# Cross scores of 18 batches in a fused cross-attention and expert block: float32 products against products of high and low halves

## The chip, the core and the metric

One Trainium2 chip, of which the kernel uses one core: TensorE (matrix products, PE in the profile), VectorE (DVE), ScalarE (ACT), GpSimd (POOL) and SyncE (SP, which issues the transfers), with 16 DMA engines. The metric is the time of one execution on the device in microseconds; the kernel before has a median of 1141.99 us of 3 runs (1141.2 to 1142.24).

## What is computed

Tokens x (8 x 112 x 512) pass a gated attention block and then a gated block of experts. The attention has queries in 16 heads of 128 channels and 8 groups of keys and values, once over the tokens themselves ("self") and once over 375 rows of context a batch ("cross"). Cut to the cross part:

```python
qx = _fp8_linear_pertensor(ln_out, wqx, wqx_scale, qx_in_scale).reshape(b, s, g, hpg, d)
qx = _ln(qx, qxln_w, qxln_b)
kvx = jnp.einsum('bsi,oi->bso', cond, w_kv_x)
kx, vx = jnp.split(kvx, 2, axis=-1)
kx = _ln(kx.reshape(b, sc, g, d), kxln_w, kxln_b)
xout = _gqa(qx, kx, vx).reshape(b, s, nh * d)      # softmax(qx kx^T * scale) vx
cat = jnp.concatenate([core, xout], axis=-1)       # core: the self part
```

cat is rounded to 8-bit floats and projected, added to x, and the experts follow. Everything is in float32, to float32's accuracy but for the roundings to 8 bits.

## The kernel before

The attention runs in four groups (gp = 0 to 3), each of 4 query heads (HP) and 2 key heads (HD = 128 channels each), and in each group over the 8 batches, so there are 32 batches (g, u). Projections of queries and own keys are made for 7 tiles of 128 tokens (TJ), those of the context for each batch. A step (s, t) projects for position s (project 0 to 5: queries, cross queries, own keys and values, and three chunks of 125 context rows) and at the same time works off the attention of the batch t before it. The order of every engine is written out by hand in its step function (ScalarE near line 713, TensorE near line 905, VectorE near line 1165), and each engine runs its instructions in that order; semaphores tie them together. The steps between two positions with a tile, (g, 0) to (g, 6), are all alike; (g, 7) has last_step.

For batch t, TensorE runs after turn(t, 3) (the first key head of the context, transposed into bank p_cross[1]): project(s, 2), score_self(t) (line 836), score_cross(t, 0) and (t, 1) (line 843), turn(t, 4) (the second key head, into p_tr[1]), project(s, 3) (line 799), turn_self (850), turn_cross(t, 0) (857, which writes p_tr[1] too), score_cross(t, 2), turn_cross(t, 1), score_cross(t, 3), project(s, 4), outputs(t, 0), turn_cross 2 and 3, project(s, 5), outputs(t, 1). ScalarE copies the transposed queries and keys out of PSUM with weight and bias (turned, lines 641 to 649: qxT, kxT), and makes exp_self (657) and exp_cross (665). VectorE finds the maxima (max_self 1094, max_cross 1108), divides by the sums (norm_self 1102, norm_cross 1114 and 1116), and copies transposed probabilities (take_self 1122, take_cross 1127). smoothed (1134) writes the result into y[t % 2]; Results.exponents and rounded (201 to 212) round it and put it into a buffer cat, which SP stores to memory (store); rounded waits for the store before it.

A cross score is one product in float32, keys of 375 rows against queries of 112:

```python
pe.matmul(p_cross[0:T, h % 2, 0:TC], qxT[:, t[1] % 2, h, :], kxT[:, h // HPG, :],
          start=True, stop=True).then_inc(sx_rdy, 1)
```

In the trace each such product is two instructions. The projections, by contrast, are already made of float32r halves (x_hi = x in float32r, x_lo = x - x_hi; hi*hi + lo*hi + hi*lo).

## Time and profile before

| | |
|---|---|
| median of 3 runs | 1141.99 us |
| the profiled execution | 1142.36 us |
| its span, first to last instruction | 1140.6 us |
| TensorE busy | 1085.6 us, 95% |
| VectorE busy | 775.2 us, 68% |
| ScalarE busy | 697.9 us, 61% |
| GpSimd busy | 500.9 us, 44% |
| attention stage | to about 788 us |

Busy times overlap between engines. A TensorE instruction's length in the trace includes the time until its result has left the array, so the lengths of neighbours overlap and what one costs is the distance from its start to the next one's. A batch is named (g, u), from 0; its times are given from the start of its score_self.

### The profile page before, as it was taken

To read this page: it belongs to the slowest core of one execution; us is meant where nothing else is said; L and a number is where in the kernel's file an instruction comes from. 1 tells how busy PE (TensorE), PEld (TensorE's weight loads), DVE (VectorE), ACT (ScalarE), POOL (GpSimd) and SP (SyncE) were. 2 spreads that over 40 slices of the span, in tenths; PEclk is the share of its full clock that TensorE was granted. 3 is DMA by queue.
4 is the path that set the end of the run, shared out by engine and by line. 5 is a ranking of instruction groups with operands and counts; after the bars stand their busy time and mean duration, and the time that the engine had idled before them with its cause. 6 is when DMAs were issued, how large, how long until landed. Compare 5 with 4: busy or idle time off the path is not lost. (4 is left out here: it accounts for less than half of the span.)

```text
span 1140.6 us, 19544 instructions
## 1 busy us (share of the span) xinstructions
PE 1085.6 (95%) x5681; PEld 896.1 (79%) x5681; DVE 775.2 (68%) x1569; ACT 697.9 (61%) x2034; POOL 500.9 (44%) x576
## 2 busy tenths in 40 slices
PE   4599999999999999999999999998999789999996
PEld 3488888888888888888888888886888667878885
DVE  7999986977776887777697766667454884655000
ACT  7668888776878856888877656762241324434432
POOL 3446565445445454545544544542000235555432
PEclk8799999999999999999999999999999889999999
DMA  7221111142111214111114111112954357673310
GB/s 267 95 81 47 51 39 43 36 170 77 43 36 47 60 35 185 47 52 38 43 36 154 48 42 40 42 35 95 333 164 163 130 160 213 187 238 96 54 43 0
DMA packets 52819, 107.39 MB, mean 94 GB/s; under 512 B 6064, under 2 KB 27056, under 8 KB 51184
## 3 DMA queue, kind: packets, MB, share of 16 engines
q1 hardware_dynamic: 48016, 97.00, 25.8%
q0 software_dynamic: 4704, 9.18, 3.6%
q8 instruction: 49, 0.80, 0.3%
q14 instruction: 50, 0.41, 0.1%
HBM read 91.48 MB, written 16.52 MB: 95 GB/s over the span
## 5 line engine op out<-in xcount | busy, mean ns | idle before, releaser
L529 POOL TENSOR_TENSOR c_lo<-c_raw,c_hi 128x500 fp32r<-128x500 f32 x96 | 123.0, 1282 | 193.0 <-ACT c_hi L582 171.4
L523 POOL TENSOR_TENSOR rs<-va,mhalf 125x2 f32<-125x2 f32 (+1 forms) x180 | 201.5, 1119 | 14.2 <-POOL va L516 0.2
L516 POOL TENSOR_TENSOR va<-ss,epst 125x2 f32<-125x2 f32 (+1 forms) x180 | 59.4, 330 | 175.0 <-DVE ss L1079 100.6
L799 PE MATMUL bank<-w_hi,c_hi 128*125 128x512 f32 x384 | 120.1, 434 | 8.9 <-ACT w_hi L577 8.0
L772 PE MATMUL bank<-w_hi,xqs 128*128 128x512 f32 (+2 forms) x464 | 111.1, 362 | 11.2 <-DVE xqs L1071 11.2
L799 PE MATMUL bank<-w_lo,c_hi 128*125 128x512 f32 x384 | 105.7, 396 | 0.1
L799 PE MATMUL bank<-w_hi,c_lo 128*125 128x512 f32 x384 | 105.3, 396 | 0.0
L772 PE MATMUL bank<-w_lo,xqs 128*128 128x512 f32 (+2 forms) x464 | 101.3, 340 | 0.1
L665 ACT ACTIVATE work<-bank,nmax 112x375 f32<-112x375 f32 x128 | 73.5, 587 | 44.2 <-DVE nmax L1108 43.9
L843 PE MATMUL bank<-kxT,qxT 128*112 128x375 f32 x256 | 96.9, 480 | 0.0
L799 PEld LDWEIGHTS bank<-w_hi,c_hi 128*125 128x125 f32 x384 | 67.0, 188 | 27.1 <-issue 8.2
L772 PEld LDWEIGHTS bank<-w_hi,xqs 128*128 128x128 f32 (+1 forms) x464 | 73.7, 189 | 17.7 <-issue 11.8
L799 PEld LDWEIGHTS bank<-w_lo,c_hi 128*125 128x125 f32 x384 | 71.5, 186 | 18.9 <-DVE w_lo L434 0.8
L799 PEld LDWEIGHTS bank<-w_hi,c_lo 128*125 128x125 f32 x384 | 71.6, 186 | 18.6
L772 PEld LDWEIGHTS bank<-w_lo,xqs 128*128 128x128 f32 (+1 forms) x464 | 75.6, 187 | 11.4 <-DVE w_lo L434 0.8
L874 PE MATMUL bank<-work 125*128 125x224 f32 x384 | 83.1, 352 | 0.0
L874 PEld LDWEIGHTS bank<-work 125*128 125x128 f32 x384 | 72.5, 189 | 0.3
L627 ACT ACTIVATE nkx<-bank 125x256 f32<-125x256 f32 x96 | 38.8, 404 | 55.4 <-PE bank L799 55.4
L1134 DVE TENSOR_TENSOR results<-bank,smg 128x448 bf16<-128x448 f32 x64 | 39.8, 622 | 46.1 <-PE bank L874 45.9
L1108 DVE TENSOR_REDUCE nmax<-bank 112x1 f32<-112x375 f32 x128 | 69.2, 543 | 2.7 <-PE bank L843 0.2
L1524 POOL DMA_INDIRECT out<-p_cat,of_row x21 | 43.6, 2075 | 58.9 <-ACT p_cat L1628 45.9
L582 ACT ACTIVATE c_hi<-c_raw 128x500 fp32r<-128x500 f32 x96 | 64.1, 668 | 1.5 <-DMA c_raw<-in_ctxT 1.5
(274 smaller groups left out, 2790.8 us busy)
## 6 DMA issues: line engine op xcount, KB each, us to landing
c_raw<-in_ctxT SPq DMA_DIRECT2D x96, 250.0 KB, 2.6
shared<-in_w_in SPq DMA_DIRECT2D x13, 1024.0 KB, 8.9
shared<-in_wproj SPq DMA_DIRECT2D x32, 256.0 KB, 4.1
raw_g<-in_Wg SPq DMA_DIRECT2D x8, 1024.0 KB, 6.5
raw_u<-in_Wu SPq DMA_DIRECT2D x8, 1024.0 KB, 6.1
raw_d<-in_Wd SPq DMA_DIRECT2D x8, 1024.0 KB, 5.5
cat_scratch<-results SPq DMA_DIRECT2D x32, 224.0 KB, 2.0
shared<-cat_scratch SPq DMA_DIRECT2D x2, 1792.0 KB, 9.9
```

The costliest lines, as they stand in the source:

```text
L516: pool.tensor_tensor(va[0:rows, lo:hi], ss[0:rows, lo:hi], epst[0:rows, lo:hi], ALU.add).then_inc(va_done, 1)
L523: pool.tensor_tensor(rs[0:rows, lo:hi], va[0:rows, lo:hi], mhalf[0:rows, lo:hi], ALU.pow).then_inc(rs_done, 1)
L529: pool.tensor_tensor(flat(c_lo[:, k, :, :]), flat(c_raw[:, k, :, :]), flat(c_hi[:, k, :, :]).bitcast(F32), ALU.subtract).then_inc(cl_done, 1)
L582: act.activation(flat(c_hi[:, k, :, :]), flat(c_raw[:, k, :, :]), ACT.Copy).then_inc(ch_done, 1)
L665: act.activation(pcross[0:T, h, :], p_cross[0:T, h % 2, 0:TC], ACT.Exp, bias=nmax[0:T, 4 + h:5 + h], accum_out=lsum[0:T, 4 + h:5 + h]).the ...
L772: m = pe.matmul(out, xqs[:, n, k, 0:rows], (w_hi, w_lo)[i // KB][:, k, lo:lo + w], start=(i == 0), stop=(i == 2 * KB - 1))
L799: m = pe.matmul(bank[0:CT, :], a[:, ch, k, :], w[:, k, CKX:CV], start=(i == 0), stop=(i == 3 * KB - 1))
L843: pe.matmul(p_cross[0:T, h % 2, 0:TC], qxT[:, t[1] % 2, h, :], kxT[:, h // HPG, :], start=True, stop=True).then_inc(sx_rdy, 1)
L874: m = pe.matmul(out[:, HPG * T:2 * HPG * T], valx[0:CT, par, k, g * P:(g + 1) * P], flat(pcrossT[0:CT, k, HPG * g:HPG * (g + 1), :]), star ...
L1108: v.tensor_reduce(nmax[0:T, 4 + h:5 + h], p_cross[0:T, h % 2, 0:TC], AX, ALU.max, negate=True).then_inc(mx_done, 1)
L1134: v.tensor_tensor(results.y[lin(t) % 2][:, g * 4 * T:(g + 1) * 4 * T].rearrange("p (a t) -> p a t", t=T), out_bank(t, g)[:, 0:4 * T].rearr ...
L1524: pool.indirect_dma_start(out=tokens[:, :], out_offset=bass.IndirectOffsetOnAxis(ap=of_row[:, 1, i:i + 1], axis=0), in_=y[:, i % 2, :], in ...
```

## The change

For the 18 batches (g, u) with g > 0 and u < 6 (has_halves), each cross score is made of three float32r products instead of one in float32: queries' low by keys' high, high by high, and queries' high by keys' low half, all into one PSUM tile; 375 columns become 376 (one of zeros). The halves are made by VectorE, with six new instructions a batch: a copy and a subtraction for the four heads' queries (halves_of_queries), and for each of two key heads a multiply-and-add straight out of the PSUM bank into kx_hi and a subtraction from kxT into kx_lo (halves_of_keys). halves_of_queries and halves_of_keys(t, 0) stand ahead of max_self, halves_of_keys(t, 1) behind norm_cross 1. TensorE's order of the steps is kept; score_cross waits for the halves, and turn_cross(t, 0), which writes the bank from which kx_hi of the second head is made, waits for that as well.

To make room, kxT has one key head instead of two (turned(t, 4) now waits for score_cross 1), pcross two heads instead of four, the results have no buffer of their own for the rounded value (the subtraction is in place, and smoothed waits for the store of two batches before), and small tiles share memory. In the last step, without projections, TensorE's turn(t, 4) moves behind the cross scores, and so does ScalarE's turned(t, 4). SP's loop over batches is unrolled.

```diff
@@ Results
-        self.held = sb(c, "results", [P, 4 * 8 * T], BF16)
-        *self.y, self.e, self.cat = (self.held[:, k * 8 * T:(k + 1) * 8 * T] for k in range(4))
+        self.held = sb(c, "results", [P, 6 * FF], BF16)
+        *self.y, self.e = (self.held[:, k * 8 * T:(k + 1) * 8 * T] for k in range(3))
+        self.rest = self.held[:, 3 * 8 * T:6 * FF]
...
-        v.wait_ge(self.stored, 16 * (t + 1))
-        v.tensor_tensor(self.cat[:, :], y[:, :], self.e[:, :], ALU.subtract).then_inc(self.ct_done, 1)
+        v.tensor_tensor(y[:, :], y[:, :], self.e[:, :], ALU.subtract).then_inc(self.ct_done, 1)
...
+def has_halves(pos):
+    return pos[0] > 0 and pos[1] < TJ - 1
+def halves_no(pos, n):
+    return 6 * ((TJ - 1) * (pos[0] - 1) + pos[1]) + n + 1
...
-    kxT = sb(c, "kxT", [P, 2, TC])
+    kxT = sb(c, "kxT", [P, TC + 1])
+    qx_hi = sb(c, "qx_hi", [P, HP, T], F32R)
+    qx_lo = sb(c, "qx_lo", [P, HP, T], F32R)
+    kx_hi = sb(c, "kx_hi", [P, TC + 1], F32R)
+    kx_lo = sb(c, "kx_lo", [P, TC + 1], F32R)
@@ SyncE
-            with sp.Fori(2, B) as b:
+            for b in range(2, B):
@@ ScalarE, turned
             if n >= 3:
-                act.activation(kxT[:, n - 3, :], turn_bank(n)[:, 0:TC], ACT.Identity, bias=b,
+                if n == 4:
+                    act.wait_ge(sx_rdy, 4 * (lin(t) + 1) + 2)
+                act.activation(kxT[:, 0:TC], turn_bank(n)[:, 0:TC], ACT.Identity, bias=b,
                                scale=w).then_inc(t_done, 1)
@@ ScalarE, exp_cross
-            act.wait_ge(tr_rdy, tr_no(before(t), 6 + h))
+            act.wait_ge(tr_rdy, tr_no(before(t), 8 + h) if h < 2 else tr_no(t, 4 + h))
@@ TensorE, bank_free
+            elif n == 6 and has_halves(t):
+                pe.wait_ge(t_done, td_no(t, 4))
+                pe.wait_ge(halves, halves_no(t, 4))
@@ TensorE, score_cross
-            pe.matmul(p_cross[0:T, h % 2, 0:TC], qxT[:, t[1] % 2, h, :], kxT[:, h // HPG, :],
-                      start=True, stop=True).then_inc(sx_rdy, 1)
+            out, kh = p_cross[0:T, h % 2, 0:TC + 1], h // HPG
+            if not has_halves(t):
+                pe.matmul(out[:, 0:TC], qxT[:, t[1] % 2, h, :], kxT[:, 0:TC], start=True, stop=True).then_inc(sx_rdy, 1)
+                return
+            pe.wait_ge(halves, halves_no(t, 2 + 2 * kh))
+            pe.matmul(out, qx_lo[:, h, :], kx_hi[:, :], start=True, stop=False)
+            pe.matmul(out, qx_hi[:, h, :], kx_hi[:, :], start=False, stop=False)
+            pe.wait_ge(halves, halves_no(t, 3 + 2 * kh))
+            pe.matmul(out, qx_hi[:, h, :], kx_lo[:, :], start=False, stop=True).then_inc(sx_rdy, 1)
@@ TensorE, step
-            if not A: turn(t, 4)
-            if not A: score_self(t)
             if A: project(s, 2, g)
-            if A and Q: score_self(t)
+            if Q: score_self(t)
             if Q: score_cross(t, 0)
             if Q: score_cross(t, 1)
-            if A and Q: turn(t, 4)
+            if Q: turn(t, 4)
@@ VectorE
+        def halves_of_queries(t):
+            if not has_halves(t):
+                return
+            whole = flat(qxT[:, t[1] % 2, :, :])
+            v.wait_ge(t_done, td_no(t, 1))
+            v.wait_ge(sx_rdy, 4 * lin(t) + 4)
+            v.tensor_copy(flat(qx_hi[:, :, :]), whole).then_inc(halves, 1)
+            v.wait_ge(halves, halves_no(t, 0))
+            v.tensor_tensor(flat(qx_lo[:, :, :]), whole, flat(qx_hi[:, :, :]).bitcast(F32),
+                            ALU.subtract).then_inc(halves, 1)
+        def halves_of_keys(t, kh):
+            if not has_halves(t):
+                return
+            v.wait_ge(t_done, td_no(t, 3 + kh))
+            v.wait_ge(sx_rdy, 4 * lin(t) + 4 + 2 * kh)
+            v.tensor_scalar(kx_hi[:, 0:TC], turn_bank(3 + kh)[:, 0:TC], vec[:, V_KXW:V_KXW + 1],
+                            vec[:, V_KXB:V_KXB + 1], ALU.mult, ALU.add).then_inc(halves, 1)
+            v.wait_ge(halves, halves_no(t, 2 + 2 * kh))
+            v.tensor_tensor(kx_lo[:, :], kxT[:, :], kx_hi[:, :].bitcast(F32), ALU.subtract).then_inc(halves, 1)
@@ VectorE, smoothed
             if lin(t) > 1:
-                v.wait_ge(results.ct_done, lin(t) - 1)
+                v.wait_ge(results.stored, 16 * lin(t))
@@ VectorE, step
+            if Q: halves_of_queries(t)
+            if Q: halves_of_keys(t, 0)
             if Q: max_self(t)
             if Q: max_cross(t, 0)
             if Q: max_cross(t, 1)
...
             if Q: norm_self(t)
             if Q: norm_cross(t, 0)
             if Q: norm_cross(t, 1)
+            if Q: halves_of_keys(t, 1)
             if spread: rounding(s[1] + 2, 0, 2, 2)
             if Q: take_self(t)
```

## Rows read from the trace of the kernel before

**Rows 1.** The page's first part: busy time, share of the span and instructions of each engine.
```profile
PE 1085.6 (95%) x5681; PEld 896.1 (79%) x5681; DVE 775.2 (68%) x1569; ACT 697.9 (61%) x2034; POOL 500.9 (44%) x576
```

**Rows 2.** Waits of TensorE from 240 to 750 us: engine, line, releaser, total, times, longest.
```profile
PE bank L857 <- DVE work L1116: 0.6, 2, 0.3
```

**Rows 3.** Windows of one step each: busy time and instructions by engine, clock, DMA share, GB/s.
```profile
505.86:529.63 23.77, 23.77 (x134) 20.06 (x133) 18.00 (x39) 19.90 (x67) 11.64 (x16) 1.00 0.16 44
715.03:738.80 23.77, 23.77 (x135) 20.06 (x134) 16.26 (x37) 15.32 (x54) 11.56 (x16) 1.00 0.16 43
```

**Rows 4.** Timeline of TensorE in one step: start, length, line, output and inputs, count.
```profile
505.86 0.94 PE L836 MATMUL bank<-kT,qT 128*112 128x112 f32 x8
506.65 1.43 PE L843 MATMUL bank<-kxT,qxT 128*112 128x375 f32 x4
...
509.16 1.08 PE L799 MATMUL bank<-w_hi,c_lo 128*125 128x512 f32 x4
510.09 1.09 PE L799 MATMUL bank<-w_lo,c_hi 128*125 128x512 f32 x4
...
511.40 0.49 PE L857 MATMUL bank<-ident,work 112*125 112x112 f32 x3
511.73 0.80 PE L843 MATMUL bank<-kxT,qxT 128*112 128x375 f32 x2
512.36 0.48 PE L857 MATMUL bank<-ident,work 112*125 112x112 f32 x3
```

**Rows 5.** Timeline of ScalarE in the same step.
```profile
503.63 0.59 ACT L649 ACTIVATE qxT<-bank,vec 128x256 f32<-128x256 f32 x1
...
505.28 0.71 ACT L641 ACTIVATE kxT<-bank,vec 128x375 f32<-128x375 f32 x1
...
506.78 0.69 ACT L582 ACTIVATE c_hi<-c_raw 128x500 fp32r<-128x500 f32 x1
507.50 0.35 ACT L657 ACTIVATE pself<-bank,nmax 112x112 f32<-112x112 f32 x1
...
509.84 0.23 ACT L665 ACTIVATION_READ_ACCUMULATOR work<-bank,nmax 112x1 f32 x1
509.93 0.69 ACT L641 ACTIVATE kxT<-bank,vec 128x375 f32<-128x375 f32 x1
```

**Rows 6.** Timeline of VectorE in the same step.
```profile
504.15 0.68 DVE L1079 TENSOR_REDUCE ss<-sq 128x4 f32<-128x512 f32 x1
506.85 0.62 DVE L1094 TENSOR_REDUCE nmax<-bank 112x4 f32<-112x448 f32 x1 [2.02 <-PE bank L836]
...
510.10 0.17 DVE L1114 RECIPROCAL linv<-lsum 112x2 f32<-112x2 f32 x1 [0.28 <-ACT work L665]
510.30 0.74 DVE L1116 TENSOR_SCALAR work<-work,linv 112x375 f32<-112x375 f32 x2
511.60 0.62 DVE L1122 COPY pselfT<-bank 112x448 f32<-112x448 f32 x1 [0.56 <-PE bank L850]
...
517.81 0.62 DVE L1134 TENSOR_TENSOR results<-bank,smg 128x448 bf16<-128x448 f32 x1 [0.29 <-PE bank L874]
```

**Rows 7.** VectorE's instructions: groups by line and form, 240 to 745 us; L1116 in this step.
```profile
L1127 DVE COPY work<-bank 125x336 f32<-125x336 f32 x84 | 40.1, 498 | 0.7 <-PE bank L857 0.7
...
L1088 DVE TENSOR_TENSOR nkx<-nkx,rs 125x256 f32<-125x256 f32 x66 | 26.8, 416 | 0.2
...
L1102 DVE TENSOR_TENSOR pself<-pself,linv 112x448 f32<-112x448 f32 x22 | 13.7, 625 | 0.8
...
L1116 DVE TENSOR_SCALAR work<-work,linv x4: 402/412/508, 510.3 to 516.5; 112x375 f32<-112x375 f32 x4
```

**Rows 8.** Timelines of VectorE, then TensorE, in batch 7 of group 2.
```profile
601.16 0.74 DVE L1116 TENSOR_SCALAR work<-work,linv 112x375 f32<-112x375 f32 x2
...
601.64 0.58 PE L857 MATMUL bank<-ident,work 112*125 112x112 f32 x3 [0.29 <-DVE work L1116]
602.05 0.80 PE L843 MATMUL bank<-kxT,qxT 128*112 128x375 f32 x2
```

More of the change, by code:

```diff
@@ L210, in rounded @@
         v.wait_ge(self.rnd, 3 * t + 3)
-        v.wait_ge(self.stored, 16 * (t + 1))
-        v.tensor_tensor(self.cat[:, :], y[:, :], self.e[:, :], ALU.subtract).then_inc(self.ct_done, 1)
+        v.tensor_tensor(y[:, :], y[:, :], self.e[:, :], ALU.subtract).then_inc(self.ct_done, 1)
     def store(self, sp, t):
         sp.wait_ge(self.ct_done, t + 1)
-        sp.dma_start(self.catd[t], self.cat[:, :]).then_inc(self.stored, 16)
+        sp.dma_start(self.catd[t], self.y[t % 2][:, :]).then_inc(self.stored, 16)
 def normed_rows(shared):
@@ L314, in attention @@
     sq = sb(c, "sq", [P, 2, 512])
-    sqx = sb(c, "sqx", [P, 2 * HD], BF16)
+    sqx = results.rest[:, 0:2 * HD]
     re = sb(c, "re", [P, 4, 2, P], BF16)
-    st = sb(c, "st", [P, TJ, 6])
     mv = sb(c, "mv", [P, TJ, 2])
@@ L323, in attention @@
     xof = sb(c, "xof", [P, 4, KB])
-    smr = sb(c, "smr", [P, GP, 8])
-    work = sb(c, "work", [P, HP * TC + 2 * NC * 256 + NC * HP * T])
-    pcross = work[:, 0:HP * TC].rearrange("p (h c) -> p h c", h=HP)
-    at = HP * TC
+    work = sb(c, "work", [P, 2 * TC + 2 * NC * 256 + NC * HP * T])
+    pcross = work[:, 0:2 * TC].rearrange("p (h c) -> p h c", h=2)
+    at = 2 * TC
     valx = work[:, at:at + 2 * NC * 256].rearrange("p (a k n) -> p a k n", a=2, k=NC)
@@ L331, in attention @@
     xs = work[:, 0:TJ * D].rearrange("p (j d) -> p j d", j=TJ)
-    ss = sb(c, "ss", [P, 16])
-    va = sb(c, "va", [P, 16])
-    rs = sb(c, "rs", [P, 16])
+    st = work[:, TJ * D:TJ * D + TJ * 6].rearrange("p (j n) -> p j n", j=TJ)
+    ss, va, rs = (results.rest[:, 2 * HD + 32 * n:2 * HD + 32 * (n + 1)].bitcast(F32) for n in range(3))
     qT = sb(c, "qT", [P, 2, HP, T])
@@ L390, in attention @@
     sx_rdy = sem(c, "sx_rdy")
+    halves = sem(c, "cross_halves")
     mx_done = sem(c, "mx_done")
@@ L455, in _ @@
         sp.dma_start(scal[:, :], scalars.partition_broadcast(P)).then_inc(vec_in, 16)
-        sp.dma_start(smr[:, :, :], smooth).then_inc(vec_in, 16)
+        sp.dma_start(smi[:, :, :], smooth).then_inc(vec_in, 16)
         for j in range(1, TJ):
@@ L496, in _ @@
         pool.memset(epst[:, :], EPS).then_inc(pool_self, 1)
+        pool.memset(kxT[:, TC:TC + 1], 0.0).then_inc(const_done, 1)
         pool.wait_ge(pool_self, 3)
@@ L662, in exp_cross @@
             act.wait_ge(mx_done, 4 * (lin(t) + 1) + h + 1)
-            act.wait_ge(tr_rdy, tr_no(before(t), 6 + h))
+            act.wait_ge(tr_rdy, tr_no(before(t), 8 + h) if h < 2 else tr_no(t, 4 + h))
             act.wait_ge(nx_done, 4 * lin(t) + h + 1)
-            act.activation(pcross[0:T, h, :], p_cross[0:T, h % 2, 0:TC], ACT.Exp,
+            act.activation(pcross[0:T, h % 2, :], p_cross[0:T, h % 2, 0:TC], ACT.Exp,
                            bias=nmax[0:T, 4 + h:5 + h], accum_out=lsum[0:T, 4 + h:5 + h]).then_inc(ex_done, 1)
@@ L707, in step @@
             if Q: turned(t, 3)
-            if not A and Q: turned(t, 4)
             if A: take(s, 1)
@@ L713, in step @@
             if Q: exp_cross(t, 1)
-            if A and Q: turned(t, 4)
+            if Q: turned(t, 4)
             if A: take(s, 2)
@@ L856, in turn_cross @@
             for k in range(NC):
-                m = pe.transpose(p_tr[0:CT, 1 - h % 2, k * T:(k + 1) * T], pcross[0:T, h, k * CT:(k + 1) * CT],
+                m = pe.transpose(p_tr[0:CT, 1 - h % 2, k * T:(k + 1) * T], pcross[0:T, h % 2, k * CT:(k + 1) * CT],
                                  ident[0:T, 0:T])
@@ L938, in step @@
             if Q: outputs(t, 1)
-        pe.wait_ge(const_done, 1)
+        pe.wait_ge(const_done, 2)
         for j in range(TJ):
@@ L1025, in constants @@
         def constants():
-            link(v.reciprocal(smi[:, :, :], smr[:, :, :]))
+            link(v.reciprocal(smi[:, :, :], smi[:, :, :]))
             for col in (V_KW, V_KB, V_KXW, V_KXB):
@@ L1115, in norm_cross @@
                 v.wait_ge(dv, CH * lin(t) + 2 + h // 2)
-            v.tensor_scalar(pcross[0:T, h, :], pcross[0:T, h, :], linv[0:T, 4 + h:5 + h], None,
+            v.tensor_scalar(pcross[0:T, h % 2, :], pcross[0:T, h % 2, :], linv[0:T, 4 + h:5 + h], None,
                             ALU.mult).then_inc(nx_done, 1)
@@ L1231, in step @@
                 inputs((s[0], s[1] + 1))
+                v.wait_ge(const_done, 2)
+                v.tensor_copy(kx_hi[:, TC:TC + 1], kxT[:, TC:TC + 1])
                 constants()
```

## The prediction

> **What bounds the kernel now.** The page's first part says that TensorE is busy 95% of the span [rows 1]. The waits of TensorE, between 240 us (just ahead of the first changed batch) and 750 us (behind the last changed scores), hold only two, 0.6 us together, and neither lies in a changed batch [rows 2]. A window over one step (23.77 us between two score_self) shows TensorE busy for all of it at a granted clock of 1.00, VectorE for 18.00, ScalarE for 19.90; a late step has the same length though VectorE and ScalarE do less [rows 3]. So TensorE's instructions set the step, and a microsecond more or less of them is a microsecond of the kernel, as long as what they wait for is there in time. Whether it is, I read from the timelines of the three engines in one step, that of batch 3 of group 2. Times below are counted from the start of its score_self, 505.86 [rows 4].
>
> **What is removed.** One head's cross scores are two instructions of 375 columns and take 0.63 us (511.73 to 512.36) [rows 4]. They become three in float32r with 376 columns. The nearest rows are c_lo's four float32r products of 512 columns, 0.93 us from one group's start to the next, 0.2325 us each [rows 4]; by columns, 0.171 us for 376, 0.512 for three. (Spacing is the price, not the duration: neighbours overlap.) Gain: 0.118 us a head, 0.47 us for four, and 72 heads would give 8.5 us if nothing waited. The lower bound of the price is half of an old instruction's 0.315, 0.158 us: then 0.475 us for three.
> The Trainium skill (TensorE: Matmul & The Clock Gate, Back-to-back issue gap) gives columns/2.4 + 2.5 ns for a matmul at full clock. That would be 0.159 us for 376 columns; its 0.216 for 512 columns is less than the 0.2325 that the trace shows for float32r, so the row is taken.
>
> **What is added, and where it waits.** Six VectorE instructions a batch. Prices by neighbours: from PSUM, 336 elements take 0.498 us, so 375 about 0.54 (keys' high half); a two-operand product in SBUF takes 0.416 for 256 and 0.625 for 448, so 376 about 0.54 (keys' low half) and 448 0.62 (queries' low half); the queries' copy is near the 0.41 of a one-operand 375, at most 0.62 [rows 7]. Together some 3.2 us, on 18.00 of 23.77 [rows 3]: VectorE isn't the bound, but its order matters.
> - *Queries.* ScalarE has written qxT at -1.64 [rows 5] and VectorE is through with sums(s, 0) at -1.03 [rows 6]. Copy and subtraction end at about 0.1 even at 0.62 each. Cost nothing: keys aren't there sooner.
> - *Keys, first head.* kxT ends at 0.13 (505.28 + 0.71) [rows 5]. With 0.03 us for each hand-over (exp_cross 1 ends at 509.84 + 0.23, the reciprocal that waits for it starts at 510.10 [rows 5, 6]) the high half runs 0.16 to 0.70, the low half 0.73 to 1.27. score_cross 0 starts at 0.79 [rows 4]: its first two products find what they need, its third, due at 1.13, waits until about 1.31. Of the 0.24 gained by heads 0 and 1 some 0.2 is lost there. That costs nothing by itself, for a longer wait follows.
> - *max_self* is queued behind the two. It started at 0.99 [rows 6]; a VectorE instruction that waits for nothing starts some 0.08 us before its predecessor's end (at 510.30 two products take 0.74 together, of 0.41 each [rows 6, 7]), so now at 1.19. exp_self started at 1.64, just when both max_self and ScalarE's work before were done; so all of exp_self, exp_cross 0 and 1, turned 4 comes 0.20 later, and norm_cross 1 ends at 5.38 in place of 5.18 [rows 5, 6].
> - *Keys, second head*, are queued behind norm_cross 1. kxT is written at 4.76 + 0.20 = 4.96 [rows 5], so they wait for VectorE alone: high half 5.30 to 5.84, low half 5.87 to 6.41. But turn_cross 0 overwrites that PSUM bank and now waits for the high half. It started at 5.54 [rows 4]; in batch 7 of group 2, where the same transposes did wait, they started 0.07 after norm_cross 0 (601.16 + 0.41; they start at 601.64), and head 2's scores 0.41 after them, not 0.33 as here [rows 4, 8]. So turn_cross 0 starts at 5.91 (0.37 late), score_cross 2 at 6.32 in place of 5.87 (0.45 late). TensorE can't fill the gap: its instructions are in order, and behind this one are all the others of the step.
> - *From there* the low half is in time (6.44 against 6.66), and heads 2 and 3 give back 2 x 0.118 = 0.24. Net **+0.21 us a step**.
> - *What is late next.* take_self waited for TensorE and started at 5.74 [rows 6]; now VectorE is through with the low half at 6.33, so the chain down to max_cross 3 is 0.6 late. It has no deadline before outputs 0 and turn_cross 2, more than 0.5 us on; before smoothed(t, 0) VectorE had 0.29 us idle [rows 6], TensorE itself is 0.2 later, and of its 5.8 idle us a step [rows 3] more lie behind. Nothing is carried to the next step.
>
> **The rest costs nothing.** One kxT in place of two: turned 4 comes after exp_cross 1, which needs score_cross 1 anyway. Two pcross in place of four: exp_cross 2 needs score_cross 2, which TensorE runs behind turn_cross 0; head 3 likewise. The results' own buffer gone: the wait for the store moves from the subtraction to smoothed two batches later, a whole step after the store; SP issues that store behind the loads of c_raw as before, unrolled or not. If its cover were gone, smoothed, and outputs behind it, would wait for a store of 224 KB. The constants' edits lie ahead of TensorE's first instruction or beside it. At the last batch turn 4 moves behind the cross scores, but head 2 waits for norm_cross 0 there too.
>
> **Sum.** 18 steps x 0.21 = +3.8 us against the profiled execution's 1142.36 (span 1140.6 and 1.76 around it): 1146.2 us. That execution is 0.37 above the median, so the median goes from 1141.99 to **1145.8 us**.
>
> **Bounds.** Each high half may take 0.41 (the one-operand SBUF row) to 0.62 us; two of them are in the path: -0.26 to +0.16 a step. The three products per head at the lower bound: -0.08 for heads 2 and 3. The restart's 0.08 may be absent. The ends are -0.21 and +0.37 a step, 1138.2 and 1148.7; the high one with subtractions at 0.62 too is 1150.
>
> **Rivals.**
> 1. *VectorE's reads of the bank are cheap.* With 0.41 us for each high half turn_cross 0 starts 0.26 sooner and the step ends 0.05 before the old one: 1141.1 us. For it: VectorE's multiply in SBUF takes that. Against it: the copy out of PSUM takes 0.498 us for 336 elements, the multiply 0.41 for 375 [rows 7].
> 2. *The other side: the wait is hidden.* If the second head's high half is visible by 5.46, when TensorE gets there, all four heads' gain stays: 72 x 0.118 = 8.5 us, 1133.5. It turns faster once the high half ends before about 5.63, 0.21 sooner than I have it. Against it: norm_cross 1, ahead of it on VectorE, alone ends at 5.18 now, and 0.5 us must follow.
> 3. *The plain rate.* At 0.158 us a product the stall stays and heads 2 and 3 give 0.31: +0.14 a step, 1144.4. The Trainium skill's gap rule, cited above, is this case.
> 4. *More is lost.* All new instructions at 0.62 us, or a second restart in the middle of score_cross 0 that delays max_cross: +0.44 a step, 1149.9.
>
> **Chances.** Forecast 0.55 (1143.5 to 1148), rival 1 0.17, rival 2 0.08, rival 3 0.12, rival 4 0.08. About 0.2% (2.3 us) is what can be told from no change: below 1139.7 is faster, above 1144.3 slower. Slower: 0.48 of the forecast, 0.07 of rival 3, rival 4: 0.63. Faster: rival 2 and 0.05 of rival 1: 0.13. Same: 0.24. The range from 1140 to 1149 leaves out rival 2, part of rival 1 and half of rival 4, some 0.17.
>
> **What the changed profile would show.** score_cross with 376 columns spaced 0.17; turn_cross 0 the top row of TensorE's waits, 18 times, on VectorE's high half, about 0.3 us idle each; TensorE's step 23.98 in place of 23.77 in 18 steps and the same in the others; exp_self 0.2 later; VectorE some 58 us busier. Wrong would be: no wait at turn_cross 0 (rival 2), high halves of 0.4 us (rival 1), steps longer by 0.4 (rival 4), or a change outside the 18 steps.

## The result: 1152.95 us, and the profile after

The changed kernel takes 1152.95 us (median of four runs, 1151.78 to 1155.17), the one before, run beside it, 1141.6 (1141.08 to 1142.24). The ratio is 1.0093 [1.0081, 1.0106]: slower by some 11 us. The forecast, 1145.8 with 1140 to 1149, has the side right and the size too small: the measured time lies outside the range. The profiled execution took 1152.14 us with a span of 1150.4, against 1142.36 and 1140.6 before: 9.8 us more.

The page's first part for the kernel after answers to [rows 1]:
```profile
PE 1089.2 (95%) x5753; PEld 908.7 (79%) x5753; DVE 831.8 (72%) x1678; ACT 698.8 (61%) x2034; POOL 511.8 (44%) x577
```
VectorE is 56.6 us busier (775.2 to 831.8; forecast 58), ScalarE does what it did.

The waits of TensorE between 240 and 760 us (engine, what waits, releaser: total, times, longest) answer to [rows 2]:
```profile
PE bank L882 <- DVE kx_hi L1132: 6.3, 18, 0.4
```
This row is new. It is the wait that the prediction named: turn_cross 0 (L882) on the keys' high half (L1132), once in each of the 18 changed batches, 0.35 us each.

A window of one step in group 2 (from one score_self to the next; length, busy time of TensorE, its weight loads, VectorE, ScalarE and GpSimd, granted clock) answers to [rows 3]:
```profile
510.06:534.39 24.33, 23.94 (x139) 20.74 (x138) 21.06 (x45) 19.92 (x67) 12.28 (x16) 1.00 0.16 42
```
From one score_self to the next it takes 24.33 us in place of 23.77; all 18 changed batches are longer by about as much, to a few hundredths, and the other steps are as before (23.75 for 23.77 in group 0). 18 x 0.56 = 10.1 us, which is the whole difference of the profiled executions (9.8). The forecast was 0.21 a step. So 0.35 us a step had to be found. The clock is 1.00 in this step on both sides and has no part in it.

The timelines of TensorE, then VectorE, in batch 3 of group 2, from score_self at 510.06 (start, length, engine, line, operation, count, and in brackets the idle time before and its releaser), answer to [rows 4] and [rows 6]:
```profile
510.06 0.95 PE L854 MATMUL bank<-kT,qT 128*112 128x112 f32 x8
511.04 0.39 PE L866 MATMUL bank<-kx_hi,qx_lo 128*112 128x376 f32 x1
511.27 0.33 PE L867 MATMUL bank<-kx_hi,qx_hi 128*112 128x376 f32 x1
511.56 0.43 PE L869 MATMUL bank<-kx_lo,qx_hi 128*112 128x376 f32 x1
511.82 0.34 PE L866 MATMUL bank<-kx_hi,qx_lo 128*112 128x376 f32 x1
512.00 0.33 PE L867 MATMUL bank<-kx_hi,qx_hi 128*112 128x376 f32 x1
512.17 0.33 PE L869 MATMUL bank<-kx_lo,qx_hi 128*112 128x376 f32 x1
...
516.33 0.55 PE L882 MATMUL bank<-ident,work 112*125 112x112 f32 x3 [0.35 <-DVE kx_hi L1132]
516.65 0.40 PE L866 MATMUL bank<-kx_hi,qx_lo 128*112 128x376 f32 x1
...
518.07 1.10 PE L814 MATMUL bank<-w_hi,c_hi 128*125 128x512 f32 x4
```
```profile
508.94 0.38 DVE L1121 CAST qx_hi<-qxT 128x448 fp32r<-128x448 f32 x1
509.36 0.62 DVE L1123 TENSOR_TENSOR qx_lo<-qxT,qx_hi 128x448 fp32r<-128x448 f32 x1
510.23 0.67 DVE L1132 TENSOR_SCALAR kx_hi<-bank,vec 128x375 fp32r<-128x375 f32 x1 [0.24 <-ACT kxT L657]
510.93 0.57 DVE L1135 TENSOR_TENSOR kx_lo<-kxT,kx_hi 128x376 fp32r<-128x376 f32 x1
511.43 0.61 DVE L1140 TENSOR_REDUCE nmax<-bank 112x4 f32<-112x448 f32 x1
...
514.87 0.74 DVE L1162 TENSOR_SCALAR work<-work,linv 112x375 f32<-112x375 f32 x2
515.53 0.66 DVE L1132 TENSOR_SCALAR kx_hi<-bank,vec 128x375 fp32r<-128x375 f32 x1
516.22 0.55 DVE L1135 TENSOR_TENSOR kx_lo<-kxT,kx_hi 128x376 fp32r<-128x376 f32 x1
```
Put beside the forecast, all counted from score_self:

| | forecast | after |
|---|---|---|
| distance of two products | 0.171 | 0.17 to 0.18 |
| keys' high half, first head | 0.16 to 0.70 | 0.17 to 0.84 |
| keys' low half, first head, ends | 1.27 | 1.44 |
| max_self starts | 1.19 | 1.37 |
| norm_cross 1 ends | 5.38 | 5.55 |
| keys' high half, second head | 5.30 to 5.84 | 5.47 to 6.13 |
| from its end to turn_cross 0 | 0.07 | 0.14 |
| turn_cross 0 starts | 5.91 | 6.27 |
| project after the four heads | 7.66 | 8.01 |

The forecast for project is its start before, 7.45 (the group behind it starts at 8.38, less 0.93 for its own four products), plus 0.21. The missing time is three terms: 0.17 from the first head's halves, handed on unchanged to norm_cross 1; 0.12 because the second high half takes 0.66 and not 0.54; 0.07 in the hand-over. Together 0.36 at turn_cross 0, and no more and no less behind it. The trace says where; it does not say why a high half takes 0.66, nor whether the first head's low half could have ended sooner. On the latter there is a row that the prediction never looked at, GpSimd's low half of the tokens, c_low (L529 before, L543 after), first in the kernel before, then after:
```profile
505.51 1.25 POOL L529 TENSOR_TENSOR c_lo<-c_raw,c_hi 128x500 fp32r<-128x500 f32 x1 [5.46 <-ACT c_hi L582]
```
```profile
509.71 1.38 POOL L543 TENSOR_TENSOR c_lo<-c_raw,c_hi 128x500 fp32r<-128x500 f32 x1 [4.98 <-ACT c_hi L596]
```
It runs from -0.35 to 0.90 before and from -0.35 to 1.03 after, right through the keys' first high half. In the changed kernel it takes 1.38 us in eight of the 18 batches and 1.26 in the other ten. The eight are those in which the queries' low half still runs when it starts (here 509.36 to 509.98, c_low at 509.71); in the ten that half is through at -0.54. In those ten (625.82 in group 3, for one) the keys' first low half takes 0.60 and ends at 1.47, the second high half ends at 6.16 and turn_cross 0 starts at 6.30: 0.03 later than in the eight. A short GpSimd addition, begun at 0.87, runs beside the start of that low half.

### The profile page after: what moved, and what is told of

Its sections match the earlier page's. It is cut to its first block and busy times, and to the rows that moved or that the text cites. A ratio compares the mean times of both kernels' runs of the same rounds, so it can differ in the third digit from the quotient of the medians.

```text
span 1150.4 us, 19476 instructions
## 1 busy us (share of the span) xinstructions
PE 1089.2 (95%) x5753; PEld 908.7 (79%) x5753; DVE 831.8 (72%) x1678; ACT 698.8 (61%) x2034; POOL 511.8 (44%) x577
## 5 line engine op out<-in xcount | busy, mean ns | idle before, releaser
L537 POOL TENSOR_TENSOR results<-results,mhalf 125x2 f32<-125x2 f32 (+1 forms) x180 | 202.2, 1123 | 14.1
L543 POOL TENSOR_TENSOR c_lo<-c_raw,c_hi 128x500 fp32r<-128x500 f32 x96 | 124.3, 1295 | 188.2 <-ACT c_hi L596 166.6
L530 POOL TENSOR_TENSOR results<-results,epst 125x2 f32<-125x2 f32 (+1 forms) x180 | 64.9, 361 | 181.8 <-DVE results L1102 111.2
L814 PE MATMUL bank<-w_hi,c_hi 128*125 128x512 f32 x384 | 114.4, 420 | 8.3 <-ACT w_hi L591 7.4
L1575 POOL DMA_INDIRECT out<-p_cat,of_row x21 | 46.2, 2199 | 58.5 <-ACT p_cat L1679 47.9
L882 PEld LDWEIGHTS bank<-ident,work 112*125 112x125 f32 x384 | 53.7, 188 | 17.1 <-issue 9.7
L882 PE MATMUL bank<-ident,work 112*125 112x112 f32 x384 | 58.8, 275 | 7.6 <-DVE kx_hi L1132 6.3
```

Source lines behind the costliest of these rows:

```text
L530: pool.tensor_tensor(va[0:rows, lo:hi], ss[0:rows, lo:hi], epst[0:rows, lo:hi], ALU.add).then_inc(va_done, 1)
L537: pool.tensor_tensor(rs[0:rows, lo:hi], va[0:rows, lo:hi], mhalf[0:rows, lo:hi], ALU.pow).then_inc(rs_done, 1)
L543: pool.tensor_tensor(flat(c_lo[:, k, :, :]), flat(c_raw[:, k, :, :]), flat(c_hi[:, k, :, :]).bitcast(F32), ALU.subtract).then_inc(cl_done, 1)
L814: m = pe.matmul(bank[0:CT, :], a[:, ch, k, :], w[:, k, CKX:CV], start=(i == 0), stop=(i == 3 * KB - 1))
L882: m = pe.transpose(p_tr[0:CT, 1 - h % 2, k * T:(k + 1) * T], pcross[0:T, h % 2, k * CT:(k + 1) * CT], ident[0:T, 0:T])
L1575: pool.indirect_dma_start(out=tokens[:, :], out_offset=bass.IndirectOffsetOnAxis(ap=of_row[:, 1, i:i + 1], axis=0), in_=y[:, i % 2, :], in ...
```

## The experiments

All edits are to the changed kernel. Steps are those of group 2 unless said otherwise. Two theories were to be told apart at first: the high halves are dear because of where they read (the PSUM bank, with weight and bias as operands), or because of what they run beside (GpSimd).

**The high half as a copy of the written kxT, e1_copy and e2_copy_wait.** Both read kxT in SBUF. The first also drops turn_cross 0's wait, since the bank is free once ScalarE has written kxT; the second keeps it.
```
-            elif n == 6 and has_halves(t):                      (e1_copy alone)
-                pe.wait_ge(t_done, td_no(t, 4))
-                pe.wait_ge(halves, halves_no(t, 4))
...
-            v.tensor_scalar(kx_hi[:, 0:TC], turn_bank(3 + kh)[:, 0:TC], vec[:, V_KXW:V_KXW + 1],
-                            vec[:, V_KXB:V_KXB + 1], ALU.mult, ALU.add).then_inc(halves, 1)
+            v.tensor_copy(kx_hi[:, 0:TC], kxT[:, 0:TC]).then_inc(halves, 1)
```


> Edit: the keys' high half is a copy of kxT in SBUF instead of a multiply-and-add out of the PSUM bank, and turn_cross 0 no longer waits for it (only for ScalarE's kxT, as before the change). Theory A (the high half out of the bank costs 0.66 us where 0.54 was forecast, stands twice in the path, and turn_cross 0 waits for its end): the copy takes about 0.35 us (448 elements take 0.39), max_self starts at about 1.05 instead of 1.37 after score_self, norm_cross 1 ends at about 5.25, turn_cross 0 doesn't wait; score_cross 2 finds both halves about in time. The step falls from 24.33 us to 23.35-23.5, below the 23.77 of the kernel before; 1134 to 1137 us. Rival B (the cost is on TensorE: three products with their own weight loads and semaphore waits are no cheaper than two in float32): the step stays above 24.1, 1148 us or more. Rival C (the smaller buffers or the moved wait for the store cost): the same, above 1148.

> Edit: the high half is a copy of kxT as in e1, but turn_cross 0 still waits for it. Separates the price of the high half from the wait itself. Theory A: the second high half ends at about 5.25 - 0.08 + 0.35 = 5.52 after score_self, turn_cross 0 starts at about 5.6 to 5.65 instead of 6.27 (it would start at 5.35 without any wait), so the step is 23.6 to 23.75 and the time 1139 to 1142 us: most of the loss is the price, the wait is worth another 3 to 6 us. Rivals B and C: above 1148 us.

Measured: e1_copy 1148.83 us, ratio to the kernel before 1.0067 [1.0045, 1.009], step 24.25; e2_copy_wait 1154.46, 1.0109 [1.0092, 1.0126], step 24.38. Both forecasts missed, and both times lie where rivals B and C would put them, so the time alone doesn't decide; the rows do, and e5_buffers and e8_stale_keys below. The top wait of TensorE in e1_copy has moved from turn_cross 0 to the first product of score_cross 0:
```profile
PE bank L863 <- DVE kx_hi L1129: 6.8, 18, 0.5
```
VectorE and GpSimd in e1_copy, score_self at 509.63:
```profile
509.80 1.08 DVE L1129 CAST kx_hi<-kxT 128x375 fp32r<-128x375 f32 x1 [0.25 <-ACT kxT L657]
...
515.48 0.35 DVE L1129 CAST kx_hi<-kxT 128x375 fp32r<-128x375 f32 x1
```
```profile
509.28 1.38 POOL L543 TENSOR_TENSOR c_lo<-c_raw,c_hi 128x500 fp32r<-128x500 f32 x1 [4.71 <-ACT c_hi L596]
```
The same instruction takes 0.35 us for the second head and 1.08 for the first. The first one begins while c_low runs; 0.35 before its end is 510.53, 0.13 before c_low's recorded end at 510.66. It was held until GpSimd was all but through and then ran at its own speed. In the batches whose c_low takes 1.26 the copy takes 0.96: the same 0.12 less. The Trainium skill (SBUF — State Buffer, Who interferes with whom) states such a thing: VectorE shares one pair of ports with GpSimd and contends for it by a copy, a cast or a tensor_scalar in its two-port mode, or by an instruction with two SBUF inputs while GpSimd reads SBUF; the engine that issues first keeps it for its whole instruction and the other is blocked. This trace agrees, but for the 0.13 us by which the copy was ahead of c_low's recorded end. So the SBUF source is cheap (0.35 against 0.66) and the gain is lost again where it meets c_low. The wait at turn_cross 0 in itself is worth 0.13 a step (24.38 against 24.25), and that was the smaller part of the loss. In e2_copy_wait TensorE waits 6.7 us at score_cross 0 as well, and the second high half ends at 6.20, later than the 6.13 of the changed kernel, although it is the shorter instruction.

**Six forms of the high half, e3_forms.** One for each group and head, to price operand and source. Where weight or bias is missing, the high half is of other numbers, and the products lose accuracy alone, since the low half makes up the rest.
```
+            form = (t[0], kh)
+            if form == (1, 0): ins = v.tensor_scalar(dst, src, w, None, ALU.mult)
+            elif form == (1, 1): ins = v.tensor_scalar(dst, src, 0.5, 0.25, ALU.mult, ALU.add)
+            elif form == (2, 0): ins = v.tensor_copy(dst, src)
+            elif form == (2, 1): ins = v.tensor_scalar(dst, kxT[:, 0:TC], w, b, ALU.mult, ALU.add)
+            elif form == (3, 0): ins = v.tensor_scalar(dst, kxT[:, 0:TC], w, None, ALU.mult)
+            else: ins = v.tensor_scalar(..., w, b, ALU.mult, ALU.add)      (bank, 374 columns)
```


> A look at what makes the high half 0.66 us. Its form differs by group and key head (the scores are then of wrong keys' high halves in all 18 batches; low halves are the rest, so the sums of halves still differ from the keys only where the high half isn't rounded right): group 1 head 0 from the bank with one pointer scalar; group 1 head 1 from the bank with two constants; group 2 head 0 a plain copy from the bank; group 2 head 1 from kxT in SBUF with two pointers; group 3 head 0 from kxT with one pointer; group 3 head 1 from the bank with two pointers and 374 columns. If the two pointer scalars are dear: 0.54 for one pointer, constants and copy from the bank, and 374 columns stay at 0.66. If the bank as source with an odd count is dear: 374 columns 0.54. If the rounding to float32r is dear: all from the bank 0.66, and the SBUF forms above 0.41.

Measured: 1149.51 us (one run). The groups of VectorE's instructions by form (busy us, mean ns of one | idle before):
```profile
L1139 DVE TENSOR_SCALAR kx_hi<-kxT,vec 128x375 fp32r<-128x375 f32 x6 | 5.7, 955 | 4.3 <-ACT kxT L657 4.3
L1140 DVE TENSOR_SCALAR kx_hi<-bank,vec 128x374 fp32r<-128x374 f32 x6 | 4.0, 660 | 0.0
L1135 DVE TENSOR_SCALAR kx_hi<-bank,vec 128x375 fp32r<-128x375 f32 x6 | 3.6, 608 | 2.4 <-ACT kxT L657 2.4
L1137 DVE CAST kx_hi<-bank 128x375 fp32r<-128x375 f32 x6 | 3.3, 548 | 2.4 <-ACT kxT L657 2.4
L1136 DVE TENSOR_SCALAR kx_hi<-bank 128x375 fp32r<-128x375 f32 x6 | 3.2, 539 | 0.0
L1138 DVE TENSOR_SCALAR kx_hi<-kxT,vec 128x375 fp32r<-128x375 f32 x6 | 2.8, 470 | 0.0
```
Out of the bank the instruction takes 0.54 us with constants or as a plain copy, 0.61 with one operand in vec, 0.66 with two; the odd column count makes no difference (374 takes the same 0.66), nor does the rounding to float32r, which the plain copy does too. So the forecast's 0.54 was right for reading PSUM and wrong for this instruction: each operand that is an address in SBUF adds some 0.06. Out of SBUF it is the same: 0.35 for the copy (e1_copy), 0.41 for norm_cross's product with one such operand [rows 7], 0.47 here with two. The top row is a first-head form from SBUF, beside c_low, at 0.955; the bottom row, with two such operands but behind c_low, takes 0.47. Group 3, which has the slow form, has the longest step:
```profile
696.62:721.18 24.56, 23.88 (x138) 20.72 (x137) 19.65 (x43) 15.35 (x54) 12.06 (x16) 1.00 0.15 42
```
Groups 1 and 2 stand at 24.20 and 24.13.

**Buffers alone, e5_buffers, and products alone, e8_stale_keys.** The first keeps the smaller buffers and runs the old scores (has_halves is False throughout). The second makes the keys' halves for the first changed batch only; the others multiply with those old keys, so the keys' four VectorE instructions and the wait at turn_cross 0 are gone from 17 batches.
```
-    return pos[0] > 0 and pos[1] < TJ - 1
+    return False                                                (e5_buffers)
...
-            if not has_halves(t):
+            if t != (1, 0):                                     (e8_stale_keys, in halves_of_keys)
                 return
```


> Edit: no batch has halves (has_halves is False); all else of the change stays: one kxT, two pcross, in-place rounding, smoothed waiting for the store, SP's loop unrolled, order of the last step. Theory A: all steps 23.77 us, 1141 to 1142.5 us. Rival C: the steps of groups 1 to 3 stay above 23.9 and the time above 1145 us.

> Left out: the keys' halves of all changed batches but the first, (1, 0); the other 17 use that batch's halves, so their scores are not theirs. The queries' halves and all three products per head stay. Shows what the products alone give on TensorE. Theory A (what is lost is lost by waiting for the keys' halves): no wait at turn_cross 0, three products cost 0.17 us each, the step is 23.77 - 0.47 = 23.3 (23.26 against the 23.73 of the kernel with the buffers alone), the time about 1132 to 1135 us. Rival B (the products are no cheaper on TensorE): 23.7 or more, above 1140 us.

Measured: e5_buffers 1143.62 us, ratio 1.0009 [0.9997, 1.0022]; e8_stale_keys 1136.0, ratio 0.9935 [0.9912, 0.9958]. Windows of a step, e5_buffers, then e8_stale_keys:
```profile
504.96:528.69 23.73, 23.73 (x134) 20.05 (x133) 18.01 (x39) 19.92 (x67) 11.63 (x16) 1.00 0.16 44
```
```profile
502.40:525.68 23.28, 23.28 (x139) 20.69 (x137) 18.83 (x41) 19.90 (x67) 12.10 (x16) 1.00 0.16 44
```
The buffers cost nothing that can be told. The products save TensorE 0.45 us a step (23.73 less 23.28; forecast 0.47), and the queries' halves, which e8_stale_keys still makes, leave that gain whole. So the change has its gain, and the keys' halves, 24.33 - 23.28 = 1.05 us a step, are the whole loss.

**The hand-over, e4_fewer_waits.** TensorE waits on two semaphores at turn_cross 0, of which the first is long due. If the 0.14 came from their number, it should fall.
```
             elif n == 6 and has_halves(t):
-                pe.wait_ge(t_done, td_no(t, 4))
                 pe.wait_ge(halves, halves_no(t, 4))
...
-            pe.wait_ge(t_done, td_no(t, 3 + h // HPG))
+            if not has_halves(t): pe.wait_ge(t_done, td_no(t, 3 + h // HPG))
```


> Edit against the changed kernel: TensorE no longer waits for ScalarE's kxT ahead of turn_cross 0 and of the changed score_cross; the wait for VectorE's high half, which itself waits for kxT, holds them. So one wait less stands ahead of the instruction that is late. In the changed kernel 0.14 us lie between the end of the second high half (6.13 after score_self) and turn_cross 0 (6.27), where 0.07 was forecast from another batch. If that is the number of waits ahead of it: 0.07 to 0.09, the step 24.33 -> 24.26 to 24.28, about 1 us less in all. If it belongs to the signal of that VectorE instruction: no change.

Measured: 1151.5 us, ratio 1.008 [1.0056, 1.0103], step 24.34. The row of the wait, TensorE:
```profile
517.35 0.55 PE L881 MATMUL bank<-ident,work 112*125 112x112 f32 x3 [0.35 <-DVE kx_hi L1131]
```
The high half ends at 517.20, the transposes start at 517.35: 0.15, as before the edit. The number of waits is not the cause.

**GpSimd out of the way of the first high half, e6_pool_after.** e1_copy, with c_low held back until the first high half is made.
```
                 for j in range(3):
+                    if j == 0 and t is not None and has_halves(t):
+                        pool.wait_ge(halves, halves_no(t, 2))
                     c_low(s, j)
```


> Edit: as e1_copy (high half copied from kxT in SBUF, no wait for it at turn_cross 0), and GpSimd's first c_low of the step waits until the first key head's high half is there. In e1 that copy took 1.08 us for the first head and 0.35 for the second; beside the first ran GpSimd's subtraction of 1.38 us. If the two engines block each other: both copies take 0.35, the first score_cross starts at 0.8 after score_self instead of 1.39, max_self at about 1.05, nothing waits long, and the step is 23.3 to 23.5; 1133 to 1137 us. If the long copy has another cause (ScalarE's writes, its place): it stays at 1.08 and the time at 1148 us.

Measured: 1144.78 us (ten runs), ratio 1.0028 [1.0017, 1.0039], step 23.95. VectorE, then GpSimd, score_self at 507.23:
```profile
507.39 0.36 DVE L1131 CAST kx_hi<-kxT 128x375 fp32r<-128x375 f32 x1 [0.23 <-ACT kxT L659]
...
511.69 1.20 DVE L1160 TENSOR_SCALAR work<-work,linv 112x375 f32<-112x375 f32 x2
```
```profile
507.82 1.63 POOL L543 TENSOR_TENSOR c_lo<-c_raw,c_hi 128x500 fp32r<-128x500 f32 x1 [5.65 <-DVE kx_hi L1131]
...
510.67 1.68 POOL L543 TENSOR_TENSOR c_lo<-c_raw,c_hi 128x500 fp32r<-128x500 f32 x1
```
The copy falls from 1.08 to 0.36 us: it was GpSimd. But the second c_low has moved too and now lies over norm_cross, whose two products take 1.20 in place of 0.74, and those stand ahead of the second high half. The collision was moved, and part of the gain went with it; the forecast (1133 to 1137) missed by 8 us for that reason: it had not asked where the held c_low would push the next one. GpSimd pays as well: its c_low takes 1.63 and 1.68, not 1.26.

**The keys ahead of the tokens, e7_keys_first.** The other way round: ScalarE writes kxT ahead of c_hi, so that the halves might be through before c_low begins; first head out of the bank, second as a copy, no wait for the bank.
```
-            if A: c_high(s, 0)
             if Q: turned(t, 3)
+            if A: c_high(s, 0)
```


> Edit: ScalarE copies the first key head out of PSUM ahead of c_high instead of behind it, so kxT is there 0.5 us sooner; its high half still comes out of the bank, that of the second head is a copy from kxT without a wait at turn_cross 0. Theory A (the time of the halves after kxT is what costs): first high half done by about 0.6, low by 1.2, max_self at about 1.1, second halves at about 5.55 and 6.15, little waiting: the step is 23.4 to 23.6, 1135 to 1139 us. Rival (it is not the start of the halves that counts, or c_low comes too late for project 3): above 1145 us.

Measured: 1154.74 us, ratio 1.0105 [1.0087, 1.0124], step 24.25, and 24.15 in group 0, where nothing had changed so far. VectorE, then GpSimd, score_self at 513.06:
```profile
512.93 0.66 DVE L1132 TENSOR_SCALAR kx_hi<-bank,vec 128x375 fp32r<-128x375 f32 x1
513.63 1.29 DVE L1135 TENSOR_TENSOR kx_lo<-kxT,kx_hi 128x376 fp32r<-128x376 f32 x1
```
```profile
513.26 1.26 POOL L543 TENSOR_TENSOR c_lo<-c_raw,c_hi 128x500 fp32r<-128x500 f32 x1 [5.50 <-ACT c_hi L596]
```
The high half came 0.30 sooner and, with c_low starting in its middle, kept its 0.66: read out of the bank it isn't held. The low half, with both inputs in SBUF, was: 1.29 in place of 0.55, and TensorE waits for it in every changed batch, 11.3 us in all. The new order on ScalarE also costs 0.4 us in steps without halves: four of group 0 (the fifth stays at 23.73), and 24.79 for 24.36 in (g, 7). A miss as a version (1135 to 1139 were forecast), but the plainest look at the second form of the collision.

**Both collisions taken away, e9_pool_twice.** e1_copy, with the first c_low behind the first head's low half and the second behind the second head's.
```
                 for j in range(3):
+                    if j < 2 and t is not None and has_halves(t):
+                        pool.wait_ge(halves, halves_no(t, (3, 5)[j]))
                     c_low(s, j)
```


> Edit: as e6_pool_after (high halves copied from kxT, no wait for them at turn_cross 0), but GpSimd's c_low 0 waits for the first key head's low half and c_low 1 for the second head's low half. In e6 the step was still 23.95 us: c_low 1 had moved to 3.44 to 5.12 after score_self and norm_cross (4.46) took 1.20 us where it takes 0.74. Theory A (each VectorE instruction between SBUF operands waits for a running GpSimd one, and nothing else is left on TensorE's path): norm_cross 0.74 again, second halves at about 5.5 and 6.05, TensorE waits only 0.1 for low halves: step 23.35 to 23.5, 1133 to 1138 us, faster than before. If c_low 1 comes too late for project 4 (due at about 8.0, it should end at 7.4), TensorE waits there instead and the time is above 1142.

Measured: 1137.55 us (1136.26 to 1138.81, five runs) against 1142.51, ratio 0.9957 [0.9943, 0.997]: faster than both kernels. As forecast (1133 to 1138, step 23.35 to 23.5). A window of a step, then VectorE, GpSimd and TensorE, score_self at 502.68:
```profile
502.68:526.16 23.48, 23.48 (x138) 20.54 (x137) 20.33 (x45) 19.89 (x67) 13.17 (x15) 1.00 0.16 44
```
```profile
502.84 0.36 DVE L1131 CAST kx_hi<-kxT 128x375 fp32r<-128x375 f32 x1 [0.20 <-ACT kxT L659]
503.23 0.55 DVE L1133 TENSOR_TENSOR kx_lo<-kxT,kx_hi 128x376 fp32r<-128x376 f32 x1
...
507.14 0.74 DVE L1160 TENSOR_SCALAR work<-work,linv 112x375 f32<-112x375 f32 x2
507.79 0.35 DVE L1131 CAST kx_hi<-kxT 128x375 fp32r<-128x375 f32 x1
```
```profile
503.86 1.26 POOL L543 TENSOR_TENSOR c_lo<-c_raw,c_hi 128x500 fp32r<-128x500 f32 x1 [6.48 <-DVE kx_lo L1133]
...
508.81 1.26 POOL L543 TENSOR_TENSOR c_lo<-c_raw,c_hi 128x500 fp32r<-128x500 f32 x1 [2.44 <-DVE kx_lo L1133]
```
```profile
503.83 0.43 PE L868 MATMUL bank<-kx_lo,qx_hi 128*112 128x376 f32 x1
504.10 0.33 PE L865 MATMUL bank<-kx_hi,qx_lo 128*112 128x376 f32 x1
```
The VectorE instructions shown are back at their own durations, c_low is at 1.26, TensorE is busy for the whole step, and the steps, 23.48 to 23.52, are 0.25 to 0.29 shorter than before the change; over the 18 batches that is 4.8 us, for a measured difference of 5.0. What is left to e8_stale_keys' 23.28 is 0.2, and it stands behind the third products of heads 0 and 2: each starts 0.05 after its low half (503.78 and 508.73), and the next product stands 0.27 and 0.26 behind it, where 0.17 is the rule. GpSimd's waits without the copy (halves out of the bank) were not run, so their share in this result isn't known by itself.

**The operands alone, e10_bank_copy.** A plain copy out of the bank, wait and GpSimd as in the changed kernel; it leaves out weight and bias in the high half.
```
-            v.tensor_scalar(kx_hi[:, 0:TC], turn_bank(3 + kh)[:, 0:TC], vec[:, V_KXW:V_KXW + 1],
-                            vec[:, V_KXB:V_KXB + 1], ALU.mult, ALU.add).then_inc(halves, 1)
+            v.tensor_copy(kx_hi[:, 0:TC], turn_bank(3 + kh)[:, 0:TC]).then_inc(halves, 1)
```


> Edit against the changed kernel: the high half is a plain copy out of the bank, without the keys' weight and bias (the high half is then of other keys, the sum of halves is not changed by it but for rounding). Gives the high half the price that was forecast: 0.55 us against 0.66 with two pointer scalars. Theory (the forecast's step failed by this price, twice in the path): turn_cross 0 starts 0.24 us sooner, 6.03 after score_self, the step is 24.09 us instead of 24.33, the time some 4.3 us less than the changed kernel's, about 1148. If the price is not in the path twice: 24.2 or more.

Measured: 1150.76 us (three runs), ratio 1.0061 [1.0043, 1.0079]. Windows of a step in group 2 and in group 3, then VectorE and GpSimd at the start of each:
```profile
508.38:532.60 24.22, 23.93 (x139) 20.74 (x138) 20.96 (x45) 19.92 (x67) 12.29 (x16) 1.00 0.15 43
719.89:743.96 24.07, 23.83 (x139) 20.73 (x138) 19.17 (x43) 15.36 (x54) 11.98 (x16) 1.00 0.15 43
```
```profile
508.54 0.55 DVE L1132 CAST kx_hi<-bank 128x375 fp32r<-128x375 f32 x1 [0.24 <-ACT kxT L657]
509.13 0.70 DVE L1134 TENSOR_TENSOR kx_lo<-kxT,kx_hi 128x376 fp32r<-128x376 f32 x1
...
720.64 0.57 DVE L1134 TENSOR_TENSOR kx_lo<-kxT,kx_hi 128x376 fp32r<-128x376 f32 x1
```
```profile
508.03 1.40 POOL L543 TENSOR_TENSOR c_lo<-c_raw,c_hi 128x500 fp32r<-128x500 f32 x1 [4.98 <-ACT c_hi L596]
...
719.55 1.26 POOL L543 TENSOR_TENSOR c_lo<-c_raw,c_hi 128x500 fp32r<-128x500 f32 x1 [5.79 <-ACT c_hi L596]
```
This run is the cleanest of all, since it holds both cases. With the price that the prediction had assumed, 0.55, the low half starts at 0.75. Where c_low takes 1.26 (group 3 and the first and last changed batch of groups 1 and 2, ten in all) it takes 0.57 and ends at 1.32, and the step is 24.07: 0.26 less than the 24.33 of the same batches in the changed kernel, 0.15 from the first head (its low half ended at 1.47 there) and 0.12 from the second. Where c_low takes 1.40 it is held to 1.45, as late as in the changed kernel (1.44), and the step is 24.20: only the second head's 0.13 comes out. The forecast of this run, 24.09 in all steps, was right for ten and missed by 0.1 for eight. So in the changed kernel the operands cost the first head some 0.13 in ten batches, and in the other eight two causes stand side by side: c_low, which the queries' low half had pushed back by 0.12, gives 1.45 without the operands' price (here), and the operands give 1.47 without the pushed c_low (the ten batches of the changed kernel).

## Why the prediction was right on the side and wrong on the size

- **What bounds the kernel**: right. 18 steps x 0.56 account for the whole difference; the other steps kept 23.75.
- **What is removed**: right. Products stand 0.17 to 0.18 apart (forecast 0.171; but 0.23 to 0.24 from the first product behind another kind to its second, and 0.26 behind a third product that had waited for its low half), and e8_stale_keys against e5_buffers shows 0.45 us a step where 0.47 was worked out. Rival 3, the plain rate of 0.158, is refuted.
- **Queries**: right for TensorE; the halves end at -0.08 (forecast about 0.1), and with them alone the gain is whole. That they push GpSimd's c_low back by 0.12 in eight batches was not foreseen; it costs nothing in the changed kernel, where the first low half is late anyway, nor in e8_stale_keys (23.27 in either kind of batch).
- **Keys, first head** is the first step that failed. Its high half was priced at 0.54 by the rows of a plain copy out of the bank, and takes 0.67: +0.13 here, and 0.04 in the start and the low half. TensorE's score_cross 0, which was to start at 0.79, starts at 0.98, 0.14 behind the high half, and its third product at 1.50 (forecast 1.31); that costs nothing by itself, as the prediction said, since TensorE is still ready for turn_cross 0 by 5.75. What the step didn't have at all is GpSimd: e10_bank_copy shows that in eight batches the end would have been the same with the price as assumed.
- **max_self and what hangs on it**: the mechanism was right. It starts 0.07 ahead of its predecessor's end (0.08 assumed), and the chain hands its delay on to norm_cross 1 unchanged, 0.17 more than forecast because the first head's end was.
- **Keys, second head** is the second step that failed, by size: 0.66 for 0.54, +0.12. e10_bank_copy gives it back (0.11 to 0.13 a step where the first head's end stays, 0.26 where it doesn't). The upper bound of 0.62 was a bound on the wrong thing: it was the dearest row of two operands in SBUF, while the operands that are addresses, weight and bias, stood in the diff and had no row with PSUM as source.
- **The hand-over to turn_cross 0**: 0.07 by [rows 8], measured 0.14, +0.07. That TensorE waits there, 18 times, and that nothing behind can fill the gap was right; the wait is 0.35 for about 0.3. The restart was put at 0.08 and costs 0.06: from turn_cross 0 to project it is 1.74 us, and 1.68 in e8_stale_keys, where nothing waits.
- **What is late next**: right. take_self is later and nothing is carried over: the delay at project, 0.35 over forecast, is that of turn_cross 0, and the step shows no other wait.
- **The rest costs nothing**: right for the buffers (e5_buffers, at 1.0009 with an interval that holds 1).
- **Rivals**: the likeliest case's mechanism held, and rival 4's size (0.44 a step, 1149.9) was nearest, but not for its reason: score_cross 0 does restart in its middle (1.50 to 1.76, 0.09 more than the rule), but max_cross follows max_self without a gap at 1.96, so that delays nothing. Rival 1, cheap reads of the bank, is refuted by 0.66. Rival 2, the gain kept, doesn't happen here (6.13 against the 5.63 that it needed), but e9_pool_twice gets there: its second high half ends at 5.46 and the profile lists no wait of TensorE in these batches.
- **The sum**: 0.21 + 0.17 + 0.12 + 0.07 = 0.57 for the measured 0.56. The profiled executions differ by 9.8 us and the medians by 11.35; in this kernel, e2_copy_wait, e5_buffers and e10_bank_copy most unprofiled runs lie up to 3 to 5 us above the profiled one. That was not explained and stays open; the causes above account for the 9.8.

What stays open too: why the hand-over takes 0.14. It does so, within 0.01, behind every form of the high half (the changed kernel, e1_copy, e4_fewer_waits, e10_bank_copy), while behind the low half TensorE starts in 0.06 (510.93 + 0.57 = 511.50, third product at 511.56). One difference is that VectorE itself waits for the high half on the same semaphore; whether that is the reason wasn't tried. It is worth 18 x 0.07 = 1.3 us.

## What to carry to other kernels

Price an added VectorE instruction by a row with the same source and the same kinds of operands; where none exists, the difference is a term of its own and widens the upper bound. Then lay the new instruction over the timeline of GpSimd as well: what VectorE reads from SBUF can be held by a GpSimd instruction that harmed nobody so long as VectorE was idle or read PSUM at that moment. If it is held, move the GpSimd instruction, and look where it lands, before moving anything on the bounding path: here the copy out of SBUF gained little by itself (+0.7% for +0.9%), and two waits on GpSimd with it made -0.4%.

## What the runs showed of the hardware

- An address operand costs VectorE time, some 0.06 us each: out of PSUM 375 columns took 0.539 us with constants, 0.608 with one, 0.660 with two (374 columns); out of SBUF 0.35 as a copy, 0.41 with one (norm_cross) and 0.470 with two.
- VectorE held by GpSimd's subtraction c_low (1.26 us): the copy from SBUF 0.35 to 1.08, the multiply with one address operand 0.955, the subtraction of two SBUF inputs 0.55 to 1.29, norm_cross's pair 0.74 to 1.20. Reads of the bank were not (0.66 to 0.67 beside it). The Trainium skill (SBUF — State Buffer, Who interferes with whom) has the rule for copies, for tensor_scalar and for two SBUF inputs, and the runs agree; the 0.955 of e3_forms is a tensor_scalar with one address operand.
- It works both ways: c_low took 1.38 to 1.40 us in place of 1.26 in just those batches in which VectorE's low half of the queries had begun before it and was still running, and 1.63 in e6_pool_after, where the keys' low half had begun 0.04 before it. Either way the late one loses some 0.14 us less than the two records overlap: the copy 0.73 of 0.86 (e1_copy), c_low 0.12 of 0.27 (the changed kernel) and 0.37 of 0.51 (e6_pool_after).
- A float32r product of 376 columns stands 0.17 to 0.18 us from the next (a head's three in 0.52), but 0.26 to 0.27 when it started 0.05 to 0.06 behind the end of the low half that it needs (511.56 to 511.82 in the changed kernel, 503.83 to 504.10 in e9_pool_twice).
